# Spreading the gates of a mixture-of-experts stage: transfers out of one SBUF row in place of products on TensorE and copies on ScalarE

## The reference

```
logits = x @ gate_w + gate_b                      # 16 experts
top_probs, top_idx = top_k(softmax(logits), 2)    # two experts a token
dispatch = one_hot(top_idx) * (top_probs / sum)   # [token, 16], 14 of 16 are zero
h1 = x @ w1[e];  h2 = x @ w2[e]                   # 64 -> 128, for every expert
out = sum over e of dispatch[token, e] * ((silu(h1) * h2) @ w3[e])
```

## Time and profile before

| | us |
|---|---|
| median of 3 runs (2575.05 to 2579.5) | 2579.14 |
| the profiled execution | 2576.05 |
| its span | 2574.2 |
| PE busy in the span | 2236.6 (87%) |
| DVE busy | 2244.8 (87%) |
| ACT busy | 1475.2 (57%) |
| POOL busy | 1767.2 (69%) |

### The profile page before, as it was taken

The page is one execution under the profiler, slowest core; times in us unless marked ns, Lnnn a source line. Parts: engine busy times, 40 slices in busy tenths (PEclk is TensorE's granted clock), DMA queues, the critical chain, the costliest instruction groups (busy, mean ns, idle before and its releaser), DMA issues.

```text
span 2574.2 us, 45353 instructions
## 1 busy us (share of the span) xinstructions
PE 2236.6 (87%) x12251; PEld 961.1 (37%) x12251; DVE 2244.8 (87%) x2638; ACT 1475.2 (57%) x3772; POOL 1767.2 (69%) x1033
## 2 busy tenths in 40 slices
PE   5558999999388989989989989899899899899878
PEld 3443333333123333333333333333333333333347
DVE  3877777777879999999999999999999999999974
ACT  0325555555146666666666666666666666666656
POOL 0112333333459889888888988888898888889843
PEclk8788999999689999999999999999999999999979
DMA  5200000000012112121211221221221212212201
GB/s 132 65 1 1 1 0 0 0 0 0 3 47 52 48 48 52 48 50 49 51 48 48 52 50 45 51 51 45 50 52 48 50 48 50 50 47 52 50 19 32
DMA packets 163216, 102.06 MB, mean 40 GB/s; under 512 B 55773, under 2 KB 161182, under 8 KB 163039
## 3 DMA queue, kind: packets, MB, share of 16 engines
q1 hardware_dynamic: 162858, 101.41, 16.0%
q10 hardware_dynamic: 316, 0.12, 0.0%
HBM read 10.63 MB, written 4.19 MB: 6 GB/s over the span
## 4 chain that ended last, share of the span: by engine, by line
PE 65%; DVE 23%; issue 9%; ACT 1%; DMA 1%; DVEq 0%; SPq 0%; POOL 0%; ACTq 0%; POOLq 0%
DVE score L1454 17%; PE pp L802 16%; PE pp L796 7%; PE pp L636 5%; PE pp L767 3%; PE pp L657 3%; PE pp L723 3%; PE pp L715 2%; PE pp L661 2%; PE pp L731 2%; PE pp L711 2%; PE pp L721 2%; PE pp L658 2%; PE pp L662 2%; PE pp L628 2%
## 5 line engine op out<-in xcount | busy, mean ns | idle before, releaser
L1454 DVE TENSOR_REDUCE score<-pp 128x16 f32<-128x1024 f32 x1408 | 1647.0, 1219 | 101.9 <-PE pp L802 82.2
L1571 POOL TENSOR_TENSOR absd<-absd 128x2560 f32<-128x2560 f32 x635 | 1442.4, 2271 | 197.1 <-ACT absd L1074 157.2
L802 PE MATMUL pp<-blocks,pick 128*128 128x512 f16 x2816 | 817.0, 383 | 155.0 <-DVE score L1454 150.4
L1074 ACT ACTIVATE absd<-pp 128x512 f32<-128x512 f32 x1280 | 695.4, 598 | 368.0 <-PE pp L796 364.1
L802 PEld LDWEIGHTS pp<-blocks,pick 128*128 128x128 f16 x2816 | 211.2, 98 | 590.7 <-DVE score L1454 421.9
L796 PE MATMUL pp<-blocks,pick 128*128 128x512 f16 x1280 | 400.0, 383 | 2.1
L1538 POOL TENSOR_TENSOR absd<-absd,yw 128x512 f32<-128x512 f32 x112 | 142.1, 1269 | 318.8 <-DVE yw L1376 318.8
L1008 ACT ACTIVATE absd<-pp 128x512 f32<-128x512 f32 x256 | 150.7, 596 | 148.1 <-PE pp L658 146.6
L1392 DVE SCALAR_TENSOR_TENSOR absd<-pp,absd 128x512 f32<-128x512 f32 x256 | 172.5, 688 | 52.9 <-ACT absd L1008 38.4
L796 PEld LDWEIGHTS pp<-blocks,pick 128*128 128x128 f16 x1280 | 119.8, 97 | 248.3 <-ACT absd L1074 84.6
L1056 ACT CAST qk<-pp 128x512 f16<-128x512 f32 x130 | 76.0, 585 | 191.2 <-PE pp L724 191.2
(11 more groups left out here) (227 smaller groups left out, 2497.9 us busy)
## 6 DMA issues: line engine op xcount, KB each, us to landing
blocks<-qk SPq DMA_DIRECT2D x1032, 64.0 KB, 2.0
attn<-score SPq DMA_DIRECT2D x1024, 16.0 KB, 1.8
xs<-xn SPq DMA_DIRECT2D x66, 32.0 KB, 1.8
big<-in_wrb_t SPq DMA_DIRECT2D x1, 2064.0 KB
big<-in_x_rows SPq DMA_DIRECT2D x4, 512.0 KB, 6.1
token_rows<-big SPq DMA_DIRECT2D x8, 256.0 KB, 2.0
big<-in_L_ffn_w SPq DMA_DIRECT2D x4, 512.0 KB, 10.1
out<-h SPq DMA_DIRECT2D x16, 128.0 KB, 2.0
```

The lines of the kernel that those rows point to most:

```text
L802: mm = pe.matmul(ps[bank + n], pick[:, unit % 8 + n, :], blocks[:, b, unit // 16, unit // 8 % 2, :], start=True, stop=True)
L1074: nc.scalar.activation(absd[odd][:, 16 * u + 8 * n:16 * u + 8 * n + 8, :], ps[4 + n].rearrange("p (h w) -> p h w", w=D), ACT.Abs).then_inc ...
L1454: dve.tensor_reduce(score[:, odd, b, 16 * d:16 * d + 16], pp[:, bank:bank + 2, :].rearrange("p n (h w) -> p (n h) w", w=D), AX.X, ALU.add, ...
L1571: nc.gpsimd.tensor_tensor(x[:, :, 0:w], x[:, :, 0:w], x[:, :, w:2 * w], ALU.add).then_inc(X["tree"], 1)
```

## The change

The gates are spread by transfers. `gT` becomes a float32 tile of 16 rows with two slots, one for each parity of the group; ScalarE's copy L999 writes it whole, and VectorE's low part goes. `gB` gets four slots and moves onto the tile `blocks`, which this stage doesn't use otherwise. SP's queue gets `spread_gates`: for each step two transfers, each of which reads one row of `gT` (one expert's 512 gates, 2 KB) 64 times and writes it to 64 partitions of the slot `k % 4`. It issues a step's transfers once that slot's last weighing is done, so four steps may be under way. Each slot has its own semaphore. The product L628, the copy L1012, the tile `both` with its load and one memset of `gT` go. The scale of 2048 leaves the gates' arithmetic.

```diff
-        both = sb("both", [64, 8, P], F16)
-        gT = sb("gT", [64, 512], F16)
+        gT = sb("gT", [EXPERTS, 2, 512])
...
-        gB = absd0[:, 3072:4096].rearrange("p (a n) -> p a n", a=2)
...
+        gB = blocks[:].rearrange("p a b c n -> p (a b c n)").bitcast(F32).rearrange("p (a n) -> p a n", a=4)
...
@@ SP's queue @@
-            sp.dma_start(both[:].rearrange("p a b -> p (a b)"), a["c_both"]).then_inc(moe_in, 16)
...
+            def spread_gates(g, b, first):
+                sp.wait_ge(C["gT"], g + 1)
+                for k in range(8):
+                    if not (first and k < 4):
+                        sp.wait_ge(C["yw"], 8 * g + k - 3)
+                    for e in range(2):
+                        row = 2 * k + e
+                        sp.dma_start(gB[64 * e:64 * e + 64, k % 4, :],
+                                     gT[row:row + 1, b, :].unsqueeze(1).to_broadcast([1, 64, 512])).then_inc(C[f"gb{k % 4}"], 16)
+
+            for b in range(2):
+                spread_gates(b, b, b == 0)
+            with sp.Fori(1, G4 // 2) as i:
+                for b in range(2):
+                    spread_gates(2 * i + b, b, False)
@@ TensorE @@
             def moe_weights(g, b):
                 pe.wait_ge(C["disp"], 3 * g + 3)
-                pe.wait_ge(C["gb"], 8 * g)
...
-            def moe_spread(g, k):
-                if k == 0:
-                    pe.wait_ge(C["gT"], 2 * g + 2)
-                elif k == 3:
-                    pe.wait_ge(C["gate"], GATE * (g + 1) + 1)
-                else:
-                    pe.wait_ge(C["gb"], 8 * g + k)
-                pe.matmul(ps[7], both[:, k, :], gT[:], start=True, stop=True).then_inc(C["gb_ps"], 1)
...
-                    moe_spread(g, k)
...
                     if k == 2:
-                        pe.wait_ge(C["gb"], 8 * g + 3)
+                        pe.wait_ge(C["gT"], g + 1)
@@ ScalarE @@
-            def moe_weights(g):
+            def moe_weights(g, b, at):
                 act.wait_ge(C["gT_ps"], g + 1)
-                act.wait_ge(C["gb_ps"], 8 * g)
-                nc.scalar.activation(gT[0:16, :], ps[7][0:16, :], ACT.Copy, scale=1.0 / LO_SCALE).then_inc(C["gT"], 1)
+                if at >= 1:
+                    act.wait_ge(C["yw"], 8 * (g - 1))
+                nc.scalar.copy(gT[:, b, :], ps[7][0:EXPERTS, :]).then_inc(C["gT"], 1)
...
-                    act.wait_ge(C["gb_ps"], n + 1)
-                    if not (first and k < 2):
-                        act.wait_ge(C["yw"], n - 1)
-                    nc.scalar.copy(gB[:, k % 2, :], ps[7]).then_inc(C["gb"], 1)
@@ VectorE @@
-            dve.memset(gT[:], 0.0).then_inc(pads, 1)
...
-                dve.tensor_scalar(disp[:, b, :, :], one, 0.5 * LO_SCALE, None, ALU.mult).then_inc(C["disp"], 1)
+                dve.tensor_scalar(disp[:, b, :, :], one, 0.5, None, ALU.mult).then_inc(C["disp"], 1)
...
-            def low_weights(g):
-                dve.wait_ge(C["gT"], 2 * g + 1)
-                dve.scalar_tensor_tensor(out=gT[32:48, :], in0=gT[0:16, :], scalar=-LO_SCALE, in1=ps[7][0:16, :],
-                                         op0=ALU.mult, op1=ALU.add).then_inc(C["gT"], 1)
...
             def weigh(g, b, k, at):
                 dve.wait_ge(C["y_ps"], 8 * g + k + 1)
-                dve.wait_ge(C["gb"], 8 * g + k + 1)
+                dve.wait_ge(C[f"gb{k % 4}"], 32 * (2 * g + k // 4 + 1))
...
-                dve.tensor_tensor(out, ps[4 + k % 2], gB[:, k % 2, :], ALU.mult).then_inc(C["yw"], 1)
+                dve.tensor_tensor(out, ps[4 + k % 2], gB[:, k % 4, :], ALU.mult).then_inc(C["yw"], 1)
```

More of the change, by code:

```diff
@@ L92, in constants @@
                 pick[3, y, g, x, y] = -1.0 / LO_SCALE
[L94 to L97, removed]
     same_head = np.kron(np.eye(16), np.ones((8, 8)))
@@ L103, in constants @@
         "c_pick": pick.reshape(P, 8 * P).astype(np.float16),
-        "c_both": both.reshape(64, 8 * P).astype(np.float16),
         "c_head": same_head.astype(np.float32),
@@ L261, in build @@
             "xs", "xT_ps", "xT_sb", "xh", "xl", "logit_ps", "logit_sb", "gate", "gap", "tanh", "disp",
-            "gT_ps", "gT", "gb_ps", "gb", "h1_ps", "h2_ps", "silu", "hid", "y_ps", "yw", "acc", "fin_ps", "sum", "eye2")}
+            "gT_ps", "gT", "gb0", "gb1", "gb2", "gb3", "h1_ps", "h2_ps", "silu", "hid", "y_ps", "yw", "acc", "fin_ps", "sum", "eye2")}
         l1_in = sem("l1_in")
@@ L358, in build @@
         ATTN_IN = 16 * 18
-        MOE_IN = 16 * 6
+        MOE_IN = 16 * 5
         L1_IN = 16 * 5
@@ L362, in build @@
         MLP_IN = 16 * 6
-        PADS = 19
+        PADS = 18
         w12_f = big2[:, 0:PAIRS * D].rearrange("p (w e n) -> p w e n", w=2, e=EXPERTS)
@@ L691, in _ @@
             pe.wait_ge(C["sum"], G4)
-            pe.wait_ge(C["gT"], 2 * G4 + 2)
+            pe.wait_ge(C["gT"], G4 + 1)
             pe.wait_ge(xn_ready[2], 1)
@@ L1018, in moe_group @@
                     if k == 7:
-                        moe_weights(g + 1)
+                        moe_weights(g + 1, 1 - b, 0 if first else 1)
             moe_x(0, 0)
@@ L1023, in _ @@
             nc.scalar.activation(gst[:, 5, :], gst[:, 4, :], ACT.Tanh, scale=0.5).then_inc(C["tanh"], 1)
-            moe_weights(0)
+            moe_weights(0, 0, 0)
             for b in range(2):
@@ L1206, in _ @@
                 dve.memset(t, 0.0).then_inc(pads, 1)
-            dve.wait_ge(pads, 14)
+            dve.wait_ge(pads, 13)
             for t in (xT4[D:D + 1, :], xT1[D:D + 1], xTq[D:D + 1, :], yT[D:D + 1, :], xT5[D:D + 1]):
@@ L1407, in moe_group @@
                             pass
-                        low_weights(g + 1)
             low_x(0, 0)
@@ L1412, in _ @@
                 pass
-            low_weights(0)
             for b in range(2):
```

## The result

The changed kernel takes 3152.0 us (3150.83 to 3152.45) against 2579.14: ratio 1.2225, 95% interval 1.2204 to 1.2246. The forecast was 3354 us in a range of 3000 to 3900.

What follows compares the result with a forecast made beforehand. Reads of one gT row, through one 27.2 GB/s way, were taken to bound the expert stage: 256 x 4.81 = 1231 us plus 2.8 and 3.5 at the ends, 1238 instead of 459.7; from 2576.05 that gives 3354 us, range 3000 to 3900.

Steps and rivals of the forecast that it cites:

- the source row's way: Expert stage: all 64 reads of a transfer queue at one 27.2 GB/s way into SBUF, 4.81 us a transfer.
- its likeliest case: Transfers queue at the source row, 4.6 to 5.6 us each: 3300 to 3560 us, chance 0.80.
- the 9.6 us a step: Expert stage: the two transfers of every step take 9.6 us together, against a TensorE step of 3.16.
- two ways at once: Rival: neighbouring transfers overlap on different ways, 2.4 us each, 2739 us in all; chance 0.03.
- The queue without gaps: SP's transfer queue in the expert stage never runs empty, so the transfers sum to 256 x 4.81 = 1231 us.
- three steps (29 us) of work: SP's queue: work still lying there when step k+4 is issued, once step k is weighed.
- A ring of any depth doesn't help.: gB's slots: a step's two rows share one port, so its 256 KB take 9.6 us whatever the depth.
- Issue hidden: SP's queue: two issues a step take 1.3 to 1.5 us, below the 3.16 us step, so they cost nothing.
- What the removal is worth: TensorE without the 128 products L628: a gain of 20 to 41 us, taken as 31, vanishing while transfers bind.
- the four steps without gating: The steps of each group of eight that gain for certain, 0.32 us each: 16 x 4 x 0.32 = 20 us.
- GB/s in its slices flat near 27: Sign that the prediction is right: the stage's transfer rate, with the DMA engines counted busy.
- TensorE busy under a third: Sign that the prediction is right: TensorE's busy share of the expert stage, forecast from about 207 to 1445 us.

Runs made afterwards that it cites:

- one_row: The changed kernel with all 256 transfers reading row 0 of gT (wrong gates): 3357.4 us, ratio 1.3016.
- cycle4: The changed kernel with expert rows reordered so that four transfers in a row read four different groups of four partitions: 2650.0 us, ratio 1.0274.
- cycle8: The changed kernel with a gT of 128 rows, each expert in eight, source rows chosen so eight transfers in a row differ in group: 2653.7 us, ratio 1.0298.
- no_transfer: The changed kernel without its 256 transfers and the wait for them, gB set to 1 once: 2556.0 us, ratio 0.9907.

## Why the prediction was right, and where it was off

- What bounds the stage. Right: the source row's way. The estimate of 4.81 us from the flat 218 GB/s of the earlier trace rows is what one_row measured, and its whole time, 3357 us, is 3 us from the forecast. The port rule of the Trainium skill ("SBUF — State Buffer", section "Door 1: The DMA port swizzle (why `[64,N]` ≈ `[32,N]`)") holds for reads in this case as well: rows 0 and 32, one port by its table, gave 3357.0 us, rows k and k + 8, two ports, 2716.
- The size. The forecast was 202 us too high, and 3152 us lies outside the 3300 to 3560 that the prediction gave its likeliest case, though inside the whole range of 3000 to 3900, in a part that no case had named. The term that was mis-sized is the 9.6 us a step, which was taken for every step: where the rows pass to a new group of four, two ways are open for some 2 us, while the old group's last transfer ends and the new group's first has begun; the step that ends there, every second one, takes 6.2 to 6.5 us. The term is 256 x 4.02 = 1029 us, not 256 x 4.81 = 1231. The rival "two ways at once" had this mechanism at full strength and gave it to another case; it was in fact part of the likeliest one.
- Do the engines drift apart? No view lists the single engines, but the trace keeps the time of each of the 16 increments by which a transfer reports its landing. The 32 increments of the first step lie within 6.4 us, those of a later step within 8.5 us (median). The next step's begin before the last of the old have come: by 1.3 us (median) where the group of four rows changes, as at 709.22 against 710.48 us, and by 0.3 us where it doesn't. With one row the increments lie even further apart, 12.2 us, and nothing is gained by it. So the shares of a transfer do end apart, and apart is worth something only where the way changes. Why they drift no run shows.
- The queue without gaps. Right: with one row 256 x 4.81 us and the ends make up the stage to within 3 us. But the queue never held the "three steps (29 us) of work" that the prediction saw in it; it held about four transfers, two steps.
- "A ring of any depth doesn't help." Right for two and four slots (3154.0 and 3152.0 us); deeper was not tried.
- Issue hidden. Right in its effect, wrong in size: a full queue makes an issue last 4.4 us. With sources on four ways this same limit, about four transfers under way, sets the time (cycle4, cycle8). I had priced the issue from rows of a queue that was never full.
- What the removal is worth. 31 us of 20 to 41; measured 23 (no_transfer), close to the lower end, which let only the four steps without gating gain. Which steps gained was not looked at.
- "GB/s in its slices flat near 27" was wrong for the changed kernel (32 in the mean, with the rhythm above), and right for one_row.
- "TensorE busy under a third" was wrong: 601 of 1039 us. It is not more work, 1924 products and transposes against 2052. At full clock they would be busy for about 416 us (an estimate: the 456.9 of the earlier trace rows less the prediction's 41), which is 34% even of the stage that was forecast, and 40% of the measured one. The rest is the clock: it was granted at 0.76 in the mean, and a product that takes 0.38 us at the upper level (2.4 GHz, granted share 1.00 from 712 to 714 us) is shown with 0.63 at the lower (1.2 GHz, 0.50 from 722 to 724 us):

```profile
712.67 0.38 PE L657 MATMUL pp<-x,absd 128*128 128x512 f16 x1
...
722.32 0.63 PE L661 MATMUL pp<-x,absd 128*128 128x512 f16 x1
```

Between 715.1 and 721.9 TensorE had started nothing. Little or none of this costs time: the weighings wait 33.3 us for TensorE (L635) against 607.7 for transfers, and a weighing that comes late by this delays no transfer, since every slot was free long before its issue.

## What to carry to other kernels

Before a broadcast is given to the DMA engines, ask how many groups of partitions its source touches: a single SBUF row was read at 27 GB/s here, with 64 targets and the 16 engines counted busy for 0.89 of the time, and four slots in the ring were worth no more than two. Write the source in several rows first (tried here: sixteen partitions, eight apart, outermost in the transfer), and the same bytes vanish behind the products. If the rows have to stay single, put those of neighbouring transfers into different groups of four partitions, not 32 apart. A landing time taken from transfers with a wide source (2.0 us) or one in HBM (2.8 us) did not carry over to one with a narrow source (15.1 us); look for a rate that halves when half of the partitions take part.

## What the runs showed of the hardware that was not expected

- SP's queue took about four transfers (3.7 to 4.4 in five kernels, 64 or 128 KB each), by their number more than by their bytes; then each issue blocked SP, for 4.4 us in the changed kernel.
- Order alone was worth 436 us: the same 256 transfers took 2.30 us each with neighbours on different ways and 4.02 us with groups of four on one.
- A transfer with two rows outermost took a DMA share of two engines, at 25 GB/s each, and its kernel was still only 84 us behind that of the same rows in two transfers with the engines at 0.91.
